# The selective scan of a Mamba-like layer: one channel tile per operation, or two

## What is computed

```python
def step(h, inp):
    x_t, dt_t, B_t, C_t = inp
    dA = jnp.exp(dt_t[..., None] * A)
    dBx = dt_t[..., None] * B_t[:, None, :] * x_t[..., None]
    h = dA * h + dBx
    y = jnp.einsum('bdn,bn->bd', h, C_t)
    return (h, y)
```

## Time and profile before

| what | us |
|---|---|
| median of three runs | 2786.01 |
| the profiled execution | 2787.32 |
| its span, first to last instruction | 2785.5 |
| mean granted clock of PE over the span | 0.936 of full |

### The profile page before, as it was taken

The page is one execution under the profiler, slowest core; times in us unless marked ns, Lnnn a source line. Parts: engine busy times, 40 slices in busy tenths (PEclk is TensorE's granted clock), DMA queues, the critical chain, the costliest instruction groups (busy, mean ns, idle before and its releaser), DMA issues. The chain is left out here.

```text
span 2785.5 us, 35722 instructions
## 1 busy us (share of the span) xinstructions
PE 2347.3 (84%) x11172; PEld 1667.8 (60%) x11172; DVE 1986.3 (71%) x3392; ACT 1475.5 (53%) x3113; POOL 1240.7 (45%) x932
## 2 busy tenths in 40 slices
PE   5966667777342899999999999999999999888997
PEld 4531111225332667777767767767777777568996
DVE  4559999994426587686686685776765866778777
ACT  2344444443102596685695685765856956842221
POOL 1129989993000364353363462543543633641122
PEclk9989999998575899999999999999999999889999
DMA  2030030000131331231231221322322312220110
GB/s 78 24 122 0 0 121 0 0 0 31 57 121 64 94 124 60 72 114 54 74 117 48 87 92 53 105 73 65 108 64 68 112 53 75 82 77 24 46 46 31
DMA packets 117376, 183.57 MB, mean 66 GB/s; under 512 B 9760, under 2 KB 77728, under 8 KB 116192
## 3 DMA queue, kind: packets, MB, share of 16 engines
q1 hardware_dynamic: 117216, 181.55, 20.3%
HBM read 170.90 MB, written 10.62 MB: 65 GB/s over the span
## 5 line engine op out<-in xcount | busy, mean ns | idle before, releaser
L78 PE MATMUL mg_pb<-xT2h,mg_wh 128*128 128x512 f32 x1152 | 483.0, 419 | 18.2 <-POOL mg_wl L1258 18.2
L79 PE MATMUL mg_pb<-xT2l,mg_wh 128*128 128x512 f32 x1152 | 458.4, 398 | 0.0
L1268 POOL TENSOR_TENSOR mg_y<-mg_hT,mg_sg 128x512 f32<-128x512 f32 x128 | 175.5, 1371 | 634.5 <-DVE mg_hT L1503 634.5
L80 PE MATMUL mg_pb<-xT2h,mg_wl 128*128 128x512 f32 x1152 | 456.5, 396 | 0.0
L778 PE MATMUL ss_y<-ss_pr,cst 128*128 128x512 f32 x512 | 294.8, 664 | 125.4 <-POOL ss_pr L763 116.5
L763 POOL TENSOR_TENSOR ss_pr<-ss_h,ss_bc 128x512 f32<-128x512 f32 x256 | 328.4, 1287 | 38.6 <-DVE ss_h L731 29.3
L1453 DVE SCALAR_TENSOR_TENSOR mg_hT<-mg_pb,mg_cw,mg_hT 128x510 f32<-128x510 f32 (+2 forms) x432 | 314.2, 740 | 32.3 <-ACT mg_hT L1608 26.5
L1480 DVE TENSOR_TENSOR mg_m<-mg_gb,mg_cb 128x384 f32<-128x384 f32 x512 | 265.2, 549 | 74.7 <-ACT mg_gb L1658 72.1
L662 ACT ACTIVATE ss_da<-dt,ss_na 128x510 f32 (+1 forms) x256 | 175.9, 689 | 210.3 <-DVE ss_h L731 210.2
L778 PEld LDWEIGHTS ss_y<-ss_pr,cst 128*128 128x128 f32 x512 | 80.7, 194 | 338.0 <-POOL ss_pr L763 330.5
L78 PEld LDWEIGHTS mg_pb<-xT2h,mg_wh 128*128 128x128 f32 x1152 | 220.4, 191 | 80.2 <-issue 18.8
(11 more groups left out here) (291 smaller groups left out, 5323.3 us busy)
## 6 DMA issues: line engine op xcount, KB each, us to landing
mg_abc<-acs_rows SPq DMA_DIRECT2D x256, 256.0 KB, 3.3
mg_ws<-in_w_in SPq DMA_DIRECT2D x72, 512.0 KB, 3.6
ss_bc<-bc_rows SPq DMA_DIRECT2D x16, 1024.0 KB, 8.5
mg_wos<-in_w_out SPq DMA_DIRECT2D x64, 256.0 KB, 4.0
ff_ws<-in_w SPq DMA_DIRECT2D x7, 1024.0 KB, 4.8
x<-in_x SPq DMA_DIRECT2D x16, 256.0 KB, 4.3
ip_ws<-in_w_in SPq DMA_DIRECT2D x8, 512.0 KB, 3.6
x_kept<-x SPq DMA_DIRECT2D x2, 2048.0 KB, 7.2
```

Of the source, the lines that this page charges most:

```text
L78: pe.matmul(out, lhs[0], rhs[0], start=start, stop=False)
L79: pe.matmul(out, lhs[0], rhs[1], start=False, stop=False)
L80: return pe.matmul(out, lhs[1], rhs[0], start=False, stop=stop)
```

## The change

One operation covers two channel tiles. `PR` = 4 pairs of tiles take the place of 8 tiles in all loops and counts, and tensors of a step become twice as wide: 1024 columns. `da`, `u` and `yb` are PSUM tensors over two banks each, `da` now with two buffers (DA = 2) in place of four, so that PSUM is filled by 2 x 2 + 2 + 2 banks. DVE's dbx, dt times x and scan and POOL's dbp and pr are one instruction per pair; the row of B or C is given to them twice by an access pattern with a zero step (`row`). ACT's decay and diagonal remain one activation per tile, since their scale is one value per channel, and signal once per pair. PE has two matmuls per step, one per bank, and signals after the second. The four buffers of h have no tensor of their own: they lie in `o`, a tensor of the surrounding scope that is free during this stage. ACT's list around a change of pair is: decay 0 of the next pair, the copy of u, decay 1, the wait for y, its copy, the diagonals, then decay 2. The zero columns at the start of each sequence are now four per buffer. Waits and counts of all engines follow from PR, DA (for `da`) and RH = 4 (for h).

```diff
--- before.py
+++ after.py
-def selective_scan(nc, sem, sb, banks, I, xc, dt, ident, bc_dram):
-    RA = 4
+def selective_scan(nc, sem, sb, banks, I, xc, dt, o, ident, bc_dram):
+    DA, RH = 2, 4
+    PR = CD // 2
+    W = 2 * HALF
...
-        dg = sb(c, "ss_dg", [P, P])
-        dbx = [sb(c, f"ss_dbx{i}", [P, HALF]) for i in range(2)]
-        us = sb(c, "ss_us", [P, HALF])
-        dbp = [sb(c, f"ss_dbp{i}", [P, HALF]) for i in range(2)]
-        hh = [sb(c, f"ss_h{i}", [P, HALF]) for i in range(RA)]
-        pr = [sb(c, f"ss_pr{i}", [P, HALF]) for i in range(2)]
-        da = banks(c, "ss_da", RA)
-        u, = banks(c, "ss_u", 1)
-        yb, = banks(c, "ss_y", 1)
+        dg = sb(c, "ss_dg", [P, 2, P])
+        dbx = [sb(c, f"ss_dbx{i}", [P, 2, HALF]) for i in range(2)]
+        us = sb(c, "ss_us", [P, 2, HALF])
+        dbp = [sb(c, f"ss_dbp{i}", [P, 2, HALF]) for i in range(2)]
+        hv = o[:].rearrange("p (i m) d -> p i (m d)", i=RH)
+        hh = [hv[:, i, :] for i in range(RH)]
+        pr = [sb(c, f"ss_pr{i}", [P, 2, HALF]) for i in range(2)]
+        wide = lambda name: c.enter_context(nc.psum_tensor(name, [P, W], F32))
+        da = [wide(f"ss_da{i}") for i in range(DA)]
+        u, yb = wide("ss_u"), wide("ss_y")
...
-        UH = CD * NST
+        UH = PR * NST
+        two = lambda t: t.rearrange("p (a t) -> p a t", a=2)
+
+        def row(n):
+            return bcb[:, n, :].unsqueeze(1).to_broadcast([P, 2, HALF])
...
         def tiles(eng, body):
-            with eng.Fori(0, CD - 1) as k:
+            with eng.Fori(0, PR - 1) as k:
                 body(k, False)
-            body(CD - 1, True)
+            body(PR - 1, True)
...
                     def decay(k, n):
                         act.wait_ge(s_h, k * NST + (half * UH + n + 1))
...
-                        act.activation(da[n % RA][:].rearrange("p (b t) -> p b t", t=SEQ)[:, :, 1:],
-                                       src[:, :, 1:], ACT.Exp,
-                                       scale=na[:, bass.ds(k, 1), n:n + 1].rearrange("p a n -> p (a n)")
-                                       ).then_inc(s_da, 1)
+                        for a in range(2):
+                            src = dt[:, bass.ds(k * 2 + a, 1), t].rearrange("p a (b t) -> p (a b) t", t=SEQ)
+                            out = da[n % DA][:, a * HALF:(a + 1) * HALF].rearrange("p (b t) -> p b t", t=SEQ)
+                            i = act.activation(out[:, :, 1:], src[:, :, 1:], ACT.Exp,
+                                               scale=na[:, bass.ds(k * 2 + a, 1), n:n + 1].rearrange("p a n -> p (a n)"))
+                        i.then_inc(s_da, 1)
...
-                        act.activation(us[:], u[:], ACT.Copy).then_inc(s_us, 1)
+                        act.activation(us[:], two(u[:]), ACT.Copy).then_inc(s_us, 1)
...
-                        act.activation(dg[:], ident, ACT.Copy, scale=dd[:, bass.ds(k, 1)]).then_inc(s_dg, 1)
+                        for a in range(2):
+                            i = act.activation(dg[:, a, :], ident, ACT.Copy, scale=dd[:, bass.ds(k * 2 + a, 1)])
+                        i.then_inc(s_dg, 1)
...
                     def body(k, last):
-                        for n in range(RA, NST):
+                        for n in range(DA, NST):
                             decay(k, n)
                         if not last:
-                            for n in range(RA - 1):
-                                decay(k + 1, n)
+                            decay(k + 1, 0)
                             copied(k + 1)
-                            decay(k + 1, RA - 1)
-                        act.wait_ge(s_y, (k + half * CD) * (NST + 1) + (2 + NST + 1))
-                        act.activation(xc[:, bass.ds(k, 1), t], yb[:].unsqueeze(1), ACT.Copy).then_inc(s_fin, 1)
+                            decay(k + 1, 1)
+                        act.wait_ge(s_y, (k + half * PR) * (NST + 1) + (2 + NST + 1))
+                        act.activation(xc[:, bass.ds(k * 2, 2), t], two(yb[:]), ACT.Copy).then_inc(s_fin, 1)
...
-                        dve.tensor_tensor(dbx[n % 2][:], u[:], bcb[:, n, :], ALU.mult).then_inc(s_dbx, 1)
+                        dve.tensor_tensor(dbx[n % 2][:], two(u[:]), row(n), ALU.mult).then_inc(s_dbx, 1)
...
-                        dve.tensor_tensor(u[:], flat(dt), flat(xc), ALU.mult).then_inc(s_u, 1)
+                        dve.tensor_tensor(two(u[:]), dt[:, bass.ds(k * 2, 2), t], xc[:, bass.ds(k * 2, 2), t], ALU.mult
+                                          ).then_inc(s_u, 1)
...
-                            dve.tensor_tensor_scan(hh[n % RA][:], da[n % RA][:], src[:], 0.0,
+                            dve.tensor_tensor_scan(hh[n % RH], da[n % DA][:], src[:].rearrange("p a t -> p (a t)"), 0.0,
                                                    ALU.mult, ALU.add).then_inc(s_h, 1)
...
-                                pool.tensor_tensor(dbp[m // BR % 2][:], us[:], bcb[:, m, :], ALU.mult
-                                                   ).then_inc(s_dbp, 1)
+                                pool.tensor_tensor(dbp[m // BR % 2][:], us[:], row(m), ALU.mult).then_inc(s_dbp, 1)
...
-                            pool.tensor_tensor(pr[n % 2][:], hh[n % RA][:], bcb[:, NST + n, :], ALU.mult
-                                               ).then_inc(s_pr, 1)
+                            pool.tensor_tensor(pr[n % 2][:], two(hh[n % RH]), row(NST + n), ALU.mult).then_inc(s_pr, 1)
...
                         for n in range(NST):
-                            pe.wait_ge(s_pr, base + (RA + n + 1))
-                            pe.matmul(yb[:], ident, pr[n % 2][:], start=False, stop=n == NST - 1
-                                      ).then_inc(s_y, 1)
+                            pe.wait_ge(s_pr, base + (RH + n + 1))
+                            for a in range(2):
+                                i = pe.matmul(yb[:, a * HALF:(a + 1) * HALF], ident, pr[n % 2][:, a, :], start=False,
+                                              stop=n == NST - 1)
+                            i.then_inc(s_y, 1)
```

More of the change, by code:

```diff
@@ L304, in build @@
                         scan_front(nc, sem, sb, banks, I, xT, xc, sz, dt, cst, eps, bc_dram, o)
-                    selective_scan(nc, sem, sb, banks, I, xc, dt, ident, bc_dram)
+                    selective_scan(nc, sem, sb, banks, I, xc, dt, o, ident, bc_dram)
                 scan_out_proj(nc, sem, sb, banks, I, xc, sz, o)
@@ L653, in _ @@
                 act.wait_ge(s_a, 2)
-                act.wait_ge(s_z, RA)
+                act.wait_ge(s_z, DA)
                 for half in range(NH):
@@ L667, in copied @@
+                        i.then_inc(s_da, 1)
                     def copied(k):
-                        act.wait_ge(s_u, k + (half * CD + 1))
+                        act.wait_ge(s_u, k + (half * PR + 1))
                         if half or not isinstance(k, int):
-                            act.wait_ge(s_dbp, k * NP + half * CD * NP)
-                        act.activation(us[:], u[:], ACT.Copy).then_inc(s_us, 1)
+                            act.wait_ge(s_dbp, k * NP + half * PR * NP)
+                        act.activation(us[:], two(u[:]), ACT.Copy).then_inc(s_us, 1)
@@ L690, in _ @@
                     copied(0)
-                    for n in range(RA):
+                    for n in range(DA):
                         decay(0, n)
                     tiles(act, body)
-                act.wait_ge(s_fin, NH * CD)
+                act.wait_ge(s_fin, NH * PR)
             @block.vector
             def _(dve):
-                dve.sem_inc(s_h, RA)
-                for i in range(RA):
+                dve.sem_inc(s_h, DA)
+                for i in range(DA):
                     dve.memset(da[i][:].rearrange("p (b t) -> p b t", t=SEQ)[:, :, 0:1], 0.0).then_inc(s_z, 1)
@@ L723, in body @@
                             if by_pool(n):
-                                dve.wait_ge(s_dbp, k * NP + (half * CD * NP + (n + 1) // BR))
+                                dve.wait_ge(s_dbp, k * NP + (half * PR * NP + (n + 1) // BR))
                                 src = dbp[n // BR % 2]
                             else:
-                                dve.wait_ge(s_dbx, k * NV + (half * CD * NV + v_count(n) + 1))
+                                dve.wait_ge(s_dbx, k * NV + (half * PR * NV + v_count(n) + 1))
                                 src = dbx[n % 2]
@@ L735, in body @@
                             if n == NST - 1 and not last:
-                                dve.wait_ge(s_us, k + (half * CD + 2))
+                                dve.wait_ge(s_us, k + (half * PR + 2))
                                 inputs(k + 1, 0)
                     dt_x(0)
-                    dve.wait_ge(s_us, half * CD + 1)
+                    dve.wait_ge(s_us, half * PR + 1)
                     inputs(0, 0)
@@ L745, in _ @@
             def _(pool):
-                pool.sem_inc(s_pr, RA)
+                pool.sem_inc(s_pr, RH)
                 for half in range(NH):
```

(23 more changed lines are left out.)

22 lines of the change are left out of this document (10 added, 12 removed).

## The result

The change makes the kernel faster by 0.9%: a median of 2761.1 us (2760.4 to 2761.9, four runs) against 2786.3 (2781.3 to 2787.3, four runs), ratio 0.9913 with a 95% interval of 0.9897 to 0.9929. The forecast was 2776.7.

A forecast was written before the change was run, and what follows sets the result against it. DVE was taken to set the stage's pace, with POOL close behind. The terms -24.3 + 1.5 + 6.0 - 1.5 + 9 = -9.3 us gave 2776.7 us from the median of 2786.0, range of 8 in 10 2763 to 2791.

The forecast's parts named there:

- 32 wide groups: DVE's four-step groups: 12.60 us wide against 13.36 for two narrow ones, 0.76 us saved each, -24.3 us.
- seven dt·x instead of fifteen: DVE's dt·x products at tile changes: one exclusion with POOL of twice the length, sum unchanged, 0 us.
- waits at the tile changes: Six wide tile changes inside the halves: third decay just in time if POOL is; 0.25 us each, +1.5 us.
- change of halves: Between the halves, nothing issued ahead: longer POOL, PE and ACT operations delay the next dbx by +3.4 us.
- end of the stage: Behind the last scan: longer POOL product, second matmul and copy of y add +2.7 us.
- rows of B and C at the start: DVE's start: waits for later rows fall away since steps are twice as long, -1.5 us.
- falls of PE's clock: PE's doubled pauses around dbp: clock falls in three groups of four delay POOL past DVE, +9 us.
- The rule by a fixed price: DVE's instruction count: a fixed 157 ns for each of 232 operations saved, estimated -36 us; the prediction argued against it.
- 11.91 + 1.08 = 12.99 us per group, more than DVE's 12.60: POOL's wide group: product time plus 0.95 us per clock fall and 0.13 restart makes POOL slower than DVE.
- Rival (b): Tile changes: two decay buffers too few, late POOL makes DVE wait at scan 2; about 2786 us, chance 0.17.
- rival (a): PE's clock holds or its falls stay within POOL's slack, so the +9 goes; 2767.7 us, chance 0.27.
- Rival (c): POOL's wide pr and dbp with the repeated row save nothing, POOL becomes the bound; 2796 to 2811 us, chance 0.14.

The follow-up runs named there:

- PE filled: Changed kernel with two zero-weight matmuls in PE's pauses after steps 3, 7 and 11 of each pair; median 2756.7 us, ratio 0.9898.
- after: The kernel after the change, against the kernel before; median 2761.1 us, ratio 0.9913.
- the split kernels: Changed kernel with wide DVE dbx products, scans, or both issued as two of 512 columns; medians 2766.2, 2765.2 and 2770.2 us.
- Run 9: Changed kernel with sixteen small memsets on POOL ahead of each dbp, PE's pauses not filled; median 2779.6 us, ratio 0.9982.
- run 12: Changed kernel issued ahead at the change of halves, PE's pauses filled, five products of sixteen on POOL instead of four; median 2770.9 us, ratio 0.9942.
- the twelve wide kernels: The changed kernel and all its variants in the follow-up runs; medians from 2751.6 to 2779.6 us.
- the halves joined and PE filled: Changed kernel issuing ahead for the second half at the change of halves, with zero-weight matmuls in PE's pauses; median 2751.6 us, ratio 0.9883.

## Why the prediction was right and wrong

The terms of the sum and what they measured, for the stage; the two with a star are taken from the kernel with PE filled, so that the clock stands in one line alone. Some terms carry tenths of a us of rounding and of the 1 us between traces.

| term | forecast | measured | from |
|---|---|---|---|
| 32 wide groups | -24.3 | -24.2 | 423.9 to 399.7 |
| seven dt·x instead of fifteen * | 0 | -4.1 | 14.8 to 10.7 |
| waits at the tile changes | +1.5 | 0 | no wait before scan 2 |
| change of halves | +3.4 | +3.1 | 3.73 to 6.81 |
| end of the stage * | +2.7 | +2.4 | 3.5 to 5.9 |
| rows of B and C at the start | -1.5 | -1.7 | 5.4 - 3.7 to 0 |
| falls of PE's clock | +9 | +4.9 | after less PE filled |
| sum | -9.3 | -19.6 | 447.6 to 428.1 is -19.5 |

**Wide operations: right.** The wide rows elsewhere were the right price, and the group came out at 12.54 us where 12.60 was forecast. That the term fits to 0.1 us is partly luck: the group's gain of 0.82 us would make 26.2 us in 32 groups. The stage gained less in this column, since the first group of a tile has one hand-over less to save, and since the overlap of 15 dt·x products, and of seven now, was taken off it (some 0.6 us). The rule by a fixed price would have said -36, and the split kernels refute it.

**Clock: mechanism right, the step after it wrong.** The falls became common as forecast, with the grant at 0.91 and 22.0 us of POOL's waits for PE. What failed is the step "11.91 + 1.08 = 12.99 us per group, more than DVE's 12.60". It takes POOL's product at 2382 ns where it was 2352 to 2369, and charges every lateness of POOL to DVE. Measured, POOL needs 5 x 2.355 = 11.8 us and 22.0 / 32 = 0.7 of waiting, together 12.5 us, just under DVE's 12.54, and over the changes of tile and of halves it catches up. No scan waited for pr, dbp or a decay. The falls reach DVE at two places alone, the dt·x product (3.8 us) and the tail (1.1). Run 9 shows a loss of 14.5 us by the falls where POOL is 0.55 us per group fuller, and even there no scan waits for pr or dbp. That step is 4.1 us of the 10.3 by which the stage's sum missed.

**The dt·x product: a term left out.** I wrote that the sum stays the same: one exclusion of twice the length for two. But the product is an instruction too, and the wait in it, which I had put at 0.5 us for a wide one, was 0.28 us with POOL on time (1.51 less 1.23). Fifteen took 14.8 us; seven wide ones take 10.7 with POOL on time. That they then took 14.5 belongs to the clock. Of the 4.1 us some 0.6 are the overlap that the other time lost, so DVE is held for 3.5 us less. In the sum this term is another 4.1 us.

**Tile changes: right that they just hold.** The third decay of the next pair was ready in time everywhere; at the change around 450 us the copy of y began at 457.50, the two activations of the decay ran from 459.00 to 460.29, and DVE, whose second scan began at 458.56, ended it at 460.84 only to take the third. The allowance of 1.5 us wasn't needed. Rival (b) lost for want of lateness: its wait is seen, in small, only where POOL had more work, once in run 9 (2.2 us) and seven times in run 12 (5.3 us).

**Range.** With the stage's -19.5 alone the median of before gives 2766.5 us, inside the range of 8 in 10 and nearest to rival (a), whose condition (falls within POOL's slack) is nearly what happened. The difference of the medians is 25.2. The other 5.7 lie outside the stage, where I had allowed nothing, though I had said that more than 3 us there would make the sum wrong. Some of it needs no cause in the change: the time ahead of the stage moves by up to 5 us with PE's grant there, whatever the kernel, and 13 more executions of the kernel before have a median of 2785.0, which makes the difference 23.9 and the part outside 4.4. Whether the change also shortens the rest stays open. Of the 15.6 us between forecast and time 10.2 are in the stage, 8.2 of them by the two steps above, the clock's and the dt·x product's, and 1.5 by the allowance at the tile changes; the part outside, whose cause isn't shown, carried the time out of the range. Rival (c) fell with the measured widths; POOL's wide product saves 8% on two narrow ones.

## What to carry to other kernels

Price a merged instruction by its start-to-start time in the stream, not by its duration: here the hand-overs from a scan to the product that waits for it, half as many now, were worth about as much as the instructions saved. Charge a delay of a second engine to the bounding one only after finding the place at which it reaches it; here those were one product in sixteen steps and the tail, and with a fuller POOL the change of halves as well. And before giving work to an engine with idle time, look for the operation that shares a port with it: 8 more POOL products in the stage cost 28 us in seven DVE products that had nothing to do with them.

## What the runs showed of the hardware

- Splitting a 1024-column fp32 DVE product in two cost 0.066 us, splitting a scan 0.049, in a stream where the second half waits for nothing. A product that waits for the scan right in front of it started 0.116 us later than a scan in its place. The scan takes 2273 to 2278 ns for 1024 columns, with PSUM inputs that span two banks.
- In the twelve wide kernels DVE's product with two SBUF inputs ended 1.08 to 1.10 us after a POOL instruction in 83 of 84 cases, with 512 columns 0.55 to 0.56 us after it. The POOL instruction behind it took up to 3.35 us instead of 2.35. In after the product had to sit out the instruction in flight; in the kernel with five products on POOL it sat out up to three back to back, with up to 7.3 us for one product. What decides whether POOL or DVE gets its turn there stays open.
- PE's clock fell behind a pause of 2.63 us here and of 1.32 us in the kernel before. Matmuls with a zero weight in the pauses raised the grant from 0.91 to 0.97 and cost nothing on the path, since PE had room. With the halves joined and PE filled the stage is 31.4 us shorter than before the change, with the change alone 19.5.
